# Attention step with the scores last, and half of the heads scored on the upper partitions

## What is computed

```
def step(carry, qkv):
    mem, zc = carry
    qs, ks, vs = qkv
    sq = elu(qs) + 1.0
    mem = mem + einsum('bhsk,bhsv->bhkv', sq, vs)
    zc = zc + (elu(ks) + 1.0).sum(axis=-2, keepdims=True)
    scores = einsum('bhsk,bhtk->bhst', qs, ks) * scale
    att_dot = einsum('bhst,bhtv->bhsv', softmax(scores), vs)
    num = einsum('bhsk,bhkv->bhsv', sq, mem)
    den = sq.sum(axis=-1, keepdims=True) * zc
    att = gate * (num / den) + (1.0 - gate) * att_dot
    return (mem, zc), att.reshape(Bx, L, H * DV) @ Wo
```

## Time and profile before

| | us |
|---|---|
| median of 3 runs (1025.58 to 1029.86) | 1029.44 |
| the profiled execution | 1023.68 |
| its span | 1021.9 |
| TensorE matmul busy | 791.6 (77%) |
| VectorE busy | 619.2 (61%) |
| ScalarE busy | 542.7 (53%) |
| GpSimd busy | 515.4 (50%) |

### The profile page before, as it was taken

One profiled execution on the slowest core, in us unless ns is written; L12 is line 12 of the kernel. 1 busy time (PEld: TensorE's weight loads), 2 busy tenths in 40 slices (PEclk: granted clock), 3 DMA queues, 4 the chain that ended last, 5 costly groups with the idle time before them and its releaser, 6 DMA issues. The chain is left out here.

```text
span 1021.9 us, 26750 instructions
## 1 busy us (share of the span) xinstructions
PE 791.6 (77%) x9501; PEld 683.3 (67%) x9502; DVE 619.2 (61%) x1217; ACT 542.7 (53%) x1119; POOL 515.4 (50%) x524
## 2 busy tenths in 40 slices
PE   5688898899988899889989899987599450099940
PEld 4577777787877778778778787877366450089940
DVE  4466666666766767666676676766588450034438
ACT  4656666656676566665676666672222110067730
POOL 2364546655565555565555645564334116546742
PEclk8788989988998989898898988998799655589985
DMA  6565655655655665565655656654118501140023
GB/s 211 133 179 137 146 135 144 144 165 144 144 144 144 165 150 138 144 144 165 156 132 144 149 161 149 138 146 123 49 32 232 64 1 44 52 107 31 31 74 111
DMA packets 115499, 127.71 MB, mean 125 GB/s; under 512 B 6913, under 2 KB 101409, under 8 KB 109329
## 3 DMA queue, kind: packets, MB, share of 16 engines
q1 hardware_dynamic: 112928, 122.17, 48.1%
q0 software_dynamic: 2544, 5.21, 1.5%
HBM read 67.42 MB, written 43.16 MB: 108 GB/s over the span
## 5 line engine op out<-in xcount | busy, mean ns | idle before, releaser
L304 POOL TENSOR_TENSOR ps<-s_exp,row_rec 128x512 f32<-128x512 f32 x64 | 66.7, 1045 | 202.5 <-DVE row_rec L669 202.5
L326 POOL TENSOR_TENSOR lhs<-pos_qv,ungate 64x1024 f32<-64x1024 f32 x64 | 150.6, 2353 | 2.5
L313 POOL TENSOR_TENSOR e_qk<-e_qk 128x512 f32<-128x512 f32 (+2 forms) x96 | 79.3, 826 | 90.0 <-DVE e_qk L637 85.0
L502 ACT ACTIVATE s_exp<-s_exp 128x512 f32<-128x512 f32 x64 | 40.2, 628 | 137.0 <-DVE s_exp L717 137.0
L645 DVE SCALAR_TENSOR_TENSOR qv_out<-bank,e_qk 128x512 f32<-128x512 f32 x64 | 44.2, 692 | 104.4 <-ACT e_qk L526 103.5
L401 PE MATMUL bank<-const,ps 128*128 128x128 f32 x512 | 94.1, 342 | 2.9 <-issue 2.5
L657 DVE TENSOR_TENSOR lhs<-mix,zg_all 64x512 f32<-64x512 f32 x128 | 88.3, 690 | 7.5 <-DMA zg_all<-scratch_z 3.6
L579 ACT ACTIVATE psT<-bank 128x512 f32<-128x512 f32 x128 | 72.4, 595 | 22.1 <-PE bank L401 21.8
L427 PE MATMUL bank<-kT,qkT 64*64 64x64 f32 x2048 | 83.0, 249 | 0.0
L372 PE MATMUL bank<-w_v,x_cur 128*128 128x512 f32 x192 | 77.7, 559 | 3.6 <-DVE w_v L603 3.6
L401 PEld LDWEIGHTS bank<-const,ps 128*128 128x128 f32 x512 | 74.3, 175 | 8.7 <-issue 3.0
(11 more groups left out here) (210 smaller groups left out, 1684.8 us busy)
## 6 DMA issues: line engine op xcount, KB each, us to landing
scratch_qv<-qv_out SPq DMA_DIRECT2D x32, 1024.0 KB, 4.0
pos_qv<-scratch_qv SPq DMA_DIRECT2D x64, 512.0 KB, 6.2
kT<-qkT SPq DMA_DIRECT2D x32, 512.0 KB, 4.1
zg_all<-scratch_z SPq DMA_DIRECT2D x64, 256.0 KB, 3.8
sorted_x<-padding SPq DMA_DIRECT2D x1, 2515.5 KB, 20.7
r_all<-in_x_dram SPq DMA_DIRECT2D x4, 512.0 KB, 6.7
cx<-in_ctx_dram SPq DMA_DIRECT2D x8, 256.0 KB, 2.8
w<-in_L_ffn_W_dram SPq DMA_DIRECT2D x1, 2048.0 KB, 9.4
```

Of the source, the lines that this page charges most:

```text
L313: pool.tensor_tensor(dst, e_qk[:, 0:c, DK:], e_qk[:, c:2 * c, DK:], ALU.add).then_inc(k_summed, 1)
L326: pool.tensor_tensor(lhs[0:L, 1 - n, :, :], pos_qv[q][s, :, DK:], ungate[s, :, :], ALU.mult).then_inc(vg_ready, 1)
```

## The change

The scores of heads 0 to 7 are done on partitions 0 to 63 as before, those of heads 8 to 15 on partitions 64 to 127: there k is already in place, and q's rows are copied up. One DMA of 512 KB becomes two of 256 KB into a new tile swapT. `score` is one function that takes the two halves in turn. It moves to the end of TensorE's step, behind all four `turn_ps`; `output` moves behind `remember` and takes batch t-2 instead of t-3; q's projection moves up, ahead of z_sum and `attend`. On VectorE sq_sum moves ahead of `cut_k`, the evacuations of the memory go one ahead of each `cut_q`, and the score part goes last. On GpSimd ps from pos_qv moves ahead of k's tree sum and stage_x goes last. On ScalarE the evacuation of the attention product moves behind q's copies, and the first exponential of a batch to the head of the next step. pos_qv has one buffer now, qv_out two.

```diff
-        qv_out = sb("qv_out", [P, C, 2 * DK])
+        qv_out = [sb(f"qv_out{i}", [P, C, 2 * DK]) for i in range(2)]
-        kT = sb("kT", [DK, P, C])
+        swapT = sb("swapT", [P, P, C])
-        pos_qv = [sb(f"pos_qv{i}", [P, H, 2 * DK]) for i in range(2)]
+        pos_qv = sb("pos_qv", [P, H, 2 * DK])
+        def heads(rows, s, hh):
+            return rows[s, :, :].rearrange("p (n g t) c -> p n g (t c)", n=SEG, g=2)[:, :, hh]
...
 SP:
                 if two:
                     sp.wait_ge(stored_qv, 16 * t)
+                    if not is_step(u, 0):
+                        sp.wait_ge(mem_ready, 2 * u)
+                        sp.wait_ge(vg_ready, 2 * u)
...
-                    sp.dma_start(kT[:, :, :], qkT[DK:, :, :]).then_inc(kT_loaded, 16)
+                    for hh in range(2):
+                        to, frm = (slice(0, DK), slice(DK, P))[::1 - 2 * hh]
+                        sp.dma_start(heads(swapT, to, hh), heads(qkT, frm, hh)).then_inc(swap_loaded, 16)
...
 PE:
                     pe.wait_ge(v_evac, t + 1)
+                    for hh in range(2):
+                        project(proj_bank, w_q, hh, q_proj)
                 if two:
-                    pe.matmul(proj_bank[0][0:SEG * H, 0:DK], cst("z_sum"), k_sum[:, :], ...)
-                if four:
-                    output(t - 3)
+                    pe.wait_ge(shifted, 2 * t - 1)
+                    pe.matmul(score_bank[0][0:SEG * H, 0:DK], cst("z_sum"), k_sum[:, :], ...)
                 if three:
                     attend(t - 2, 0)
                     attend(t - 2, 1)
                 if one:
-                    project(proj_bank, w_q, 0, q_proj)
-                    project(proj_bank, w_q, 1, q_proj)
                     for f in range(4):
                         turn_qk(f)
                 if two:
                     remember(0)
                     remember(1)
-                    turn_ps(0)
-                    turn_ps(1)
-                if one:
-                    score(0)
-                    score(1)
-                if two:
-                    turn_ps(2)
-                    turn_ps(3)
+                if three:
+                    output(t - 2)
+                if two:
+                    for f in range(4):
+                        turn_ps(f)
+                if one:
+                    score()
...
+                def score():
+                    pe.wait_ge(qkT_evac, 4 * t + 4)
+                    pe.wait_ge(swap_loaded, 32 * (t + 1))
...
                     for i in range(8):
+                        for hh in range(2):
+                            s = slice(hh * DK, (hh + 1) * DK)
+                            q_rows, k_rows = (qkT, swapT)[::1 - 2 * hh]
+                            for n in range(SEG):
+                                tok = n * L + J * (8 * hh + i)
+                                last = pe.matmul(score_bank[hh][n * L:(n + 1) * L, i * L:(i + 1) * L],
+                                                 q_rows[s, tok:tok + J, :], k_rows[s, tok:tok + J, :], ...)
...
 DVE:
+                if two:
+                    dve.wait_ge(qv_loaded, 32 * t)
+                    if not is_step(u, 0):
+                        dve.wait_ge(sqn_ready, u)
+                    dve.tensor_reduce(sq_sum[:, :], pos_qv[:, :, 0:DK], X, ALU.add).then_inc(sq_summed, 1)
+                    dve.wait_ge(sq_summed, t)
+                    dve.reciprocal(sq_rec[:, :], sq_sum[:, :]).then_inc(sq_inv, 1)
                 if one:
                     cut_k(0)
-                if not is_step(t, 0, 1, 2):
-                    residual(t - 3)
-                if one:
                     cut_k(1)
                 if not is_step(t, 0, 1):
                     move_att(t - 2)
                 if two:
-                    (sq_sum and its reciprocal, as above)
+                    evac_memory(0)
                 if one:
                     cut_q(0)
                 if two:
-                    evac_memory(0)
+                    evac_memory(1)
                 if one:
                     cut_q(1)
-                if two:
-                    evac_memory(1)
+                if not is_step(t, 0, 1):
+                    residual(t - 2)
+                if two:
+                    evac_memory(2)
+                    evac_memory(3)
                 if one:
                     (maximum and shift of the scores, two halves)
-                if two:
-                    evac_memory(2)
-                    evac_memory(3)
```

More of the change, by code:

```diff
@@ L325, in step @@
                         s = slice(n * L, (n + 1) * L)
-                        pool.tensor_tensor(lhs[0:L, 1 - n, :, :], pos_qv[q][s, :, DK:], ungate[s, :, :], ALU.mult).then_inc(vg_ready, 1)
+                        pool.tensor_tensor(lhs[0:L, 1 - n, :, :], pos_qv[s, :, DK:], ungate[s, :, :], ALU.mult).then_inc(vg_ready, 1)
                         pool.wait_ge(vg_ready, 2 * u + n + 1)
+                if one:
+                    stage_x(t + 1, 1 - p)
             run_steps(pool, step, B, peeled=2)
@@ L358, in output @@
                 for c in range(C // 2):
-                    last = pe.matmul(proj_bank[1][:, 0:D], attT[:, c, :], w_o[:, c, :], start=(c == 0), stop=(c == C // 2 - 1))
+                    last = pe.matmul(score_bank[1][:, 0:D], attT[:, c, :], w_o[:, c, :], start=(c == 0), stop=(c == C // 2 - 1))
                 last.then_inc(out_ready, 1)
@@ L450, in step @@
                         pe.wait_ge(const_loaded, 16)
-                    if not one:
-                        pe.wait_ge(sq_ready, 2 * t)
+                    pe.wait_ge(shifted, 2 * t - 1)
                     pe.wait_ge(k_summed, 4 * t)
-                    pe.matmul(proj_bank[0][0:SEG * H, 0:DK], cst("z_sum"), k_sum[:, :], start=True, stop=True).then_inc(zc_ready, 1)
-                if four:
-                    if is_step(t, 3):
-                        pe.wait_ge(wo_loaded, 16)
-                    output(t - 3)
+                    pe.matmul(score_bank[0][0:SEG * H, 0:DK], cst("z_sum"), k_sum[:, :], start=True, stop=True).then_inc(zc_ready, 1)
                 if three:
@@ L692, in step @@
                 if two:
-                    dve.wait_ge(qv_loaded[q], 32 * (hq + 1))
-                    if not is_step(u, 0):
-                        dve.wait_ge(sqn_ready, u)
-                    dve.tensor_reduce(sq_sum[:, :], pos_qv[q][:, :, 0:DK], X, ALU.add).then_inc(sq_summed, 1)
-                    dve.wait_ge(sq_summed, t)
-                    dve.reciprocal(sq_rec[:, :], sq_sum[:, :]).then_inc(sq_inv, 1)
+                    evac_memory(0)
                 if one:
```

97 lines of the change are left out of this document (40 added, 57 removed).

## The result

The changed kernel takes 1076.03 us (median of 4 runs, 1075.26 to 1076.65) against 1027.51 for the kernel before: ratio 1.0473, 95% interval 1.0439 to 1.0506. The forecast was 1076. The profiled execution took 1075.26 us, its span is 1073.4.

The account below looks back on a forecast made before the run. The DRAM round trip of q and v was to bind: 21.86 us plus 0.9 of low clock, 22.76 a step against 21.25; 31 periods add 47 us to 1023.7, plus 5.8 for the median: 1076, range 1034 to 1102.

Parts of the forecast that it names:

- The loop: From one cut_q(1) end to the next through DRAM: 21.86 us at full clock, 22.76 with low clock; chance 0.50.
- The landing: Loads of pos_qv: second issued 0.85 us after the first, landed 7.1 later, together 7.95 us; called unsure.
- The clock: At remember on TensorE: low clock after a hole adds 0.9 us to 2.23, bounds 0 and 1.3.
- Nearly always: On TensorE: remember starts in the low clock nearly always, after a hole of 5 to 6 us.
- One sign: On VectorE: idle before sq_sum, released by the pos_qv DMA, about 5 us a step.
- close but not late: On GpSimd: stage_x, last, ends by E + 25 (E: cut_q(1)'s end), when v's projection needs it; no cost.
- The waits added on SP for the single pos_qv: On SP: they ask for things ready by E + 2 (E: cut_q(1)'s end), load issued E + 4.3; no cost.
- z's trip ahead of `evac_memory(0)`: On SP's queue: z_sum done at E + 9 (E: cut_q(1)'s end), trip over well ahead of E + 19.
- The rule on transposes: On TensorE: if transposes don't count as clock activity, remember pays the full 1.3 us; step 23.16, 1088 us.
- TensorE as the bound: Rival: TensorE's chain, not the DRAM trip, binds; 19.5 us a step, 975 us, if the second load lands 2.3 earlier; 0.10.
- The clock low at v, k and q too: Rival: on TensorE low clock reaches these projections behind turn_ps and scores; 23.6 us a step, 1102 us; chance 0.15.
- the expected gain: On TensorE: the seeming prize, wait for k's copy 1.8 us and clock loss 1.93, some 3.7 a step.

Follow-up runs that it names:

- attend_twice: Changed kernel with each attend product issued twice, same values into the same places, 64 more TensorE passes a step; 1071.33 us.
- rows_low: Changed kernel with all scores on partitions 0 to 63 again, one DMA of k's rows, head halves still in turn; 1071.24 us.
- x_first: Changed kernel with stage_x back at the head of GpSimd's step, sq_sum left where the change put it; 1081.9 us.
- sum_late: Changed kernel with sq_sum and its reciprocal behind move_att instead of ahead of cut_k, nothing else; 1050.56 us.
- sum_late_x_first: Changed kernel with sq_sum and its reciprocal behind move_att and stage_x back at the head of GpSimd's step; 1004.09 us.
- half_load: Changed kernel loading back only heads 0 to 7 of q and v from the second load on, so output is not the layer's; 949.82 us.
- split_ps_first: Kernel before with the row split and the scores last, its other orders and both pos_qv buffers kept; 954.43 us.

## Why the prediction was right

**The loop.** The forecast named the round trip of q and v through DRAM as the bound, closed by sq_sum's new place, and summed it to 22.76 us a step; measured 22.75. The terms, in the round shown above: store issued after 0.19 us (0.19 forecast), loads issued after 4.26 (4.07; the next round has 3.90), landed after 7.96 (7.95), sq_sum and reciprocal to `cut_k` 1.42 (1.58), `cut_k` 1.26 (1.41), `move_att` 1.40 (1.40), `remember` from the end of `move_att` to the next instruction of VectorE 4.17 (2.40 at full clock, up to 3.7), evacuations and `cut_q` 2.86 (2.86). The landing was the weightiest term, and it could be read before only by asking for one step: the median over both loads, 6.2 us, hides that the second one lands last in every step (6.9 to 7.8 us after its issue, the first 5.1 to 5.8).

**The clock.** The mean of `remember` was 104.1 / 32 = 3.25 us, 1.02 over its 2.23, where I had taken 0.9. My upper bound of 1.3 was too low: the rows I took it from give 2.23 * 3.45 / 2.08 = 3.70, 1.47 over, and fully in the low clock it took 3.88, 1.65 over. "Nearly always" was wrong too: `remember` ran wholly at full clock in 9 steps of 32, wholly in the low clock in 14, and in between in the rest. The terms that were slightly large (0.3 us) made up for it, so the exact hit on the step is partly luck. So is the hit on the time. From the profiled execution of before to that of the changed kernel the span grew by 51.5 us. The 31 periods account for 46.7 of it; the other 4.8 lie ahead of the first score (1.6) and behind the last (3.2), where I had allowed 2. And I had added 5.8 us because the median of before lay that far above its profiled execution; in the changed kernel the distance is 0.8. These two errors of some 5 us cancel, which is luck.

One sign was also off: VectorE is idle 2.8 us a step before sq_sum, not the 5 I had given.

How well the loop describes the time is seen across runs. A step less the mean of `remember` should be the same in all kernels that keep the loop: it is 22.75 - 3.25 = 19.50 after the change, 22.68 - 3.03 = 19.65 in attend_twice, 22.68 - 3.20 = 19.48 in rows_low, 23.04 - 3.47 = 19.57 in x_first. The forecast's own figure is 21.86 - 2.23 = 19.63. These four kernels differ in TensorE's work by up to 2 us a step and in `remember` by 0.4, and only the second shows.

**What was reckoned at nothing.** The copy is hidden but for 6.7 us: right. The scores: the two halves overlap and are busy 38.2 us each in 32 steps, 1.2 us a step against 2.08 for the 64 passes on one row group, and irrelevant, as rows_low shows. With the rule of the Trainium skill (TensorE: Matmul & The Clock Gate, Part 3: Packing small matmuls), that tiles in different row groups run side by side, this trace agrees: 1.2 us, if not quite the half. GpSimd "close but not late": right, and it was the next bound by a hair, sum_late. The waits added on SP for the single pos_qv: next to nothing. From the store to the load it takes 4.12 us on average against 4.05 before, and SP waits 10.1 us in all for lhs. In sum_late, where lhs comes late against the load, it is 4.62. z's trip ahead of `evac_memory(0)`: right in the changed kernel (3.2 us in all), but with less slack than my sentence suggested; with `remember` earlier it became part of the loop that binds sum_late_x_first.

**The rule on transposes** of the Trainium skill (the same page, Part 4: PE-mode transpose) would have given 1088. The clock did fall behind a stretch of transposes alone, and `remember` was often wholly in the low clock, but not always, 3.25 on average against 3.88. A stretch of pure transposes long enough to decide the rule isn't in these runs.

**The rivals.** TensorE as the bound (19.5 a step): false for the changed kernel, by attend_twice and rows_low. Yet half_load shows its price was fair, even high: with the landing shortened, the same order of TensorE gives 18.92. Its condition, a landing 2.3 us earlier, was the right one. The clock low at v, k and q too: not seen. The three are busy 158.7 us in all in the changed kernel, against 183.0 before.

**Where the expected gain went.** Both halves of the change are sound. On the orders of before, the scores last are worth 5.6% and the split 2.7%. The changed kernel gives up both, and is 4.7% slower on top. Its own bound is that sq_sum stands 2.7 us of VectorE's work too early, which puts `cut_k`, `move_att` and `remember` behind a load that takes 8.0 us to land. Undoing that alone gave back 25 of the 122 us between the changed kernel and split_ps_first, and undoing stage_x's move as well 72. The other 50 lie in the rest of the new order. There z's trip beside the load closes a loop of 20.4 us, which fits the step; its share wasn't measured by itself, nor were the wait of the scores for `residual` and the single pos_qv, which by the distance from store to load (4.16 us on average) costs some 0.1 us a step there.

## What to carry to other kernels

When an order is rewritten, look for what is now in series with a transfer that runs from one step into the next: add up the loop from its own end back to its own end, landing included, and compare it with the present step. A transfer with 3 us of slack can become the bound; an instruction that reads it should stand behind what doesn't need it. Test the parts of a change singly: here two parts that were worth 5.6% and 2.7% were hidden by the rest.

## What was not expected of the hardware

- A longer loop body cost more than its instructions: with 512 more in a body of two steps there were 138 instruction packets instead of 15, and TensorE stood still 26 times, for up to 5.7 us; with 256 more there were 18 and no such waits.
- A store of 8 KB that is issued while a 1 MB load from DRAM runs lands about when the load does, after 4.3 us in the steps shown, from SP's queue and from ScalarE's alike (medians 3.7 and 4.2); its median in the kernel before was 2.0.
- Putting the scores last cut TensorE's wait ahead of them from 1.95 to 0.8 us a step, and the mean granted clock rose from 0.90 to 0.98; the step fell by 0.8 us more than the wait that went. The order of the transposes around the wait changed with it, and no run separates the two.
